# A four-layer gated cross-attention kernel: the first attention prepared three batches deep with squares on ScalarE and scaling on GpSimd, and two mixtures reordered

## The reference, cut to what matters

```python
x = x + tanh(g_xattn[0]) * L0_xattn(ctx, layernorm(x), mask)   # 4 heads of 64, layer norms, RMS norms
x = x + tanh(g_ffn[0])   * L0_ffn(layernorm(x))                # top-1 of 8 experts, hidden 1024
...
x = x + tanh(g_xattn[3]) * L3_xattn(layernorm(x), ctx)
x = x + tanh(g_ffn[3])   * L3_ffn(layernorm(x))                # 64 slots, GRU update, slot attention
```

```python
xn, ln = layernorm(ctx), layernorm(layernorm(x))        # 361 and 100 rows
q = ln @ Wq.T
k, v = split(concat([xn @ Wkv.T, ln @ Wlkv.T]))         # 461 rows: keys from context and from x
qn = q / rms(q) * q_gain * 64**-0.5                     # rms per row and head of 64
kn = k / rms(k) * k_gain
out = softmax(where(mask, qn @ kn.T, -max)) @ v @ Wo.T + bo
```

## Time and profile before

| | us |
|---|---|
| median of three runs | 2035.22 |
| lowest and highest | 2031.48, 2040.41 |
| the profiled execution: its own time | 2037.1 |
| the profiled execution: its span, first to last instruction | 2035.2 |
| PE busy in the span | 1688.3 (83%) |
| DVE busy | 1009.2 (50%) |
| ACT busy | 619.9 (30%) |
| POOL busy | 251.4 (12%) |
| mean granted clock of PE | 0.904 |

### The profile page before, as it was taken

How to read it: one execution, slowest core, us unless ns; L and a number is a source line. 1 busy time by engine, 2 the same in 40 slices (tenths; PEclk the granted TensorE clock), 3 DMA queues, 4 the chain that set the end, 5 groups by cost and what they waited for, 6 DMA issues and landing times.

```text
span 2035.2 us, 30717 instructions
## 1 busy us (share of the span) xinstructions
PE 1688.3 (83%) x9090; PEld 1185.3 (58%) x9090; DVE 1009.2 (50%) x3131; ACT 619.9 (30%) x1731; POOL 251.4 (12%) x299
## 2 busy tenths in 40 slices
PE   2888888873699993999999989979997996887676
PEld 1555545543589982666666657757775534665454
DVE  3677777754122221444444443644444555775663
ACT  1343334321222221333333323223332003443232
POOL 2222222211200003000000000110000011112000
PEclk9899889785799996999999988989998996998787
DMA  3000000700788851000000000010000003000001
GB/s 89 13 14 12 12 12 13 221 1 29 258 305 319 303 215 49 12 12 11 11 11 11 6 1 8 17 32 22 22 22 1 13 20 119 27 27 1 0 1 33
DMA packets 88389, 117.17 MB, mean 58 GB/s; under 512 B 16418, under 2 KB 80130, under 8 KB 83202
## 3 DMA queue, kind: packets, MB, share of 16 engines
q1 hardware_dynamic: 86274, 113.06, 17.2%
q0 software_dynamic: 2048, 3.29, 0.6%
HBM read 104.51 MB, written 8.52 MB: 56 GB/s over the span
## 4 chain that ended last, share of the span: by engine, by line
PE 56%; issue 21%; DVE 8%; POOL 7%; ACT 3%; DMA 1%; SPq 1%; DVEq 1%; POOLq 0%; ACTq 0%
PE bank L1811 7%; PE bank L2061 6%; PE bank L1918 5%; PE bank L2158 5%; PE bank L1868 5%; PE bank L1892 4%; PE bank L2071 4%; POOL work L645 3%; PE bank L1946 3%; PE bank L1903 3%; PE bank L1860 3%; PE bank L2113 2%; PE bank L2129 2%; PE bank L2245 2%; POOL work L638 1%
## 5 line engine op out<-in xcount | busy, mean ns | idle before, releaser
L812 ACT ACTIVATE work<-bank,work 100x361 f32<-100x361 f32 (+1 forms) x272 | 159.5, 590 | 276.7 <-DVE work L1185 225.8
L1918 PEld LDWEIGHTS bank<-work 128*100 128x100 f32 x1760 | 191.4, 174 | 76.1 <-issue 35.2
L1194 DVE COPY work<-bank 128x300 f32<-128x300 f32 (+1 forms) x272 | 125.6, 490 | 187.9 <-PE bank L1903 187.6
L1918 PE MATMUL bank<-work 128*100 128x64 f32 (+1 forms) x1760 | 198.1, 262 | 22.7 <-DVE work L1194 22.6
L2061 PEld LDWEIGHTS bank<-work 128*128 128x128 f32 x1280 | 148.4, 194 | 1.9 <-ACT work L910 0.9
L2061 PE MATMUL bank<-work 128*128 128x128 f32 x1280 | 148.7, 277 | 0.5 <-ACT work L910 0.5
L1185 DVE TENSOR_REDUCE work<-bank 100x1 f32<-100x361 f32 x208 | 101.9, 528 | 87.4 <-PE bank L1892 72.6
L1892 PE MATMUL bank<-work 64*100 64x361 f32 (+1 forms) x512 | 142.2, 558 | 2.0 <-ACT work L802 1.1
L1903 PE MATMUL bank<-ident,work 100*128 100x100 f32 x880 | 112.7, 259 | 29.2 <-ACT work L812 28.4
L638 POOL TENSOR_TENSOR work<-work,neg_half 100x1 f32<-100x1 f32 x96 | 53.2, 554 | 593.9 <-DVE work L1132 593.8
L1903 PEld LDWEIGHTS bank<-ident,work 100*128 100x128 f32 x880 | 89.8, 147 | 56.8 <-ACT work L812 49.9
(11 more groups left out here) (286 smaller groups left out, 2824.0 us busy)
## 6 DMA issues: line engine op xcount, KB each, us to landing
work<-in_F_w SPq DMA_DIRECT2D x60, 1024.0 KB, 6.4
work<-in_ctxT SPq DMA_DIRECT2D x64, 135.4 KB, 2.2
work<-in_ctx SPq DMA_DIRECT2D x32, 192.0 KB, 2.4
sorted_x<-zeros SPq DMA_DIRECT2D x1, 2560.0 KB, 10.0
work<-sorted_x SPq DMA_DIRECT2D x20, 128.0 KB, 6.2
work<-in_F_b SPq DMA_DIRECT2D x20, 128.0 KB, 6.7
sorted_y<-work SPq DMA_DIRECT2D x20, 128.0 KB, 6.3
work<-in_ctx SPq DMA_DIRECT2D x32, 78.8 KB, 2.2
```

The source lines that it names most:

```text
L812: nc.scalar.activation(pr[:, 0:NK], S_bank[k][0:T, 0:NK], ACT.Exp, bias=nmax[k][0:T, :], accum_out=rsum[j][0:T, h:h + 1]).then_inc(s.exped ...
L1194: nc.vector.tensor_copy(PT[k][:, 0:CH, :], PT_bank[k][:, 0:CH * T].rearrange("p (c t) -> p c t", c=CH)).then_inc(s.probs_copied.sem, 1)
L1918: ins = nc.tensor.matmul(to, PT[k][:, c, :], values, start=(c == 0), stop=(c == CH - 1))
```

## The change

1. **First attention.** `three_deep` takes the place of `pipelined` there: in `first_attend(t)` steps 0 to 7 belong to batch t+2 and steps 8 to 10 to batch t+1; the norms on DVE and POOL belong to batch t+3. The order of the steps is the tuple `AHEAD`. `V` now holds four batches (`vv0`). Heads go in pairs, 0 with 1 and 2 with 3. ACT squares each chunk from PSUM before it copies it. POOL multiplies each chunk with its power right behind the power. DVE keeps the sums and their scaling.
2. **Routed mixture.** The down product of tile i-1 stands in tile i behind piece f = 1, its bias on DVE behind piece 2; `AC` has two buffers; the next rows are turned behind piece 4. SP asks for the rows of a tile before its W1. For the first two tiles W1 of both and W2 of the first are asked before SP waits for the scatter.
3. **Slot mixture.** `in_waves` takes the place of the rounds: stage s of pair u runs in wave s + 9u on every engine. `pick` works on one pair, and both additions of the logits' bias (`biased`) stand before all picks. The same instructions are issued otherwise.

The core of the diff:

```diff
-PAIRS = (0, 4, 2, 0)
-EARLY = ((0, 1), (0, 1, 2), (0, 1, 2), (0, 1, 2))
+PAIRS = (2, 4, 2, 0)
+EARLY = ((0, 1, 5), (0, 1, 2), (0, 1, 2), (0, 1, 2))
 GROUPS = (
-    ((2, 3, 4), (5, 6, 7), (), (8, 9, 10)),
+    ((2, 6, 8, 3), (4, 9, 10, 7)),
...
+AHEAD = (0, 1, 5, 2, 6, 8, 3, 4, 9, 10, 7)
+ALONE = tuple(n for n in AHEAD if n < 8)
+APART_BY = 9
+PICKED = 7
...
+def three_deep(eng, attend, finish):
+    for t in range(4):
+        attend(t, t)
+    with eng.Fori(1, B // 4 - 1) as i:
+        for q in range(4):
+            attend(4 * i + q, q)
+    for t in range(B - 4, B):
+        attend(t, t % 4)
+    finish(B - 1, 1)
+def in_waves(stages):
+    for wave in range(max(stages) + APART_BY * (B // 2 - 1) + 1):
+        for u in range(B // 2):
+            if wave - APART_BY * u in stages:
+                stages[wave - APART_BY * u](u, u % SLOTS_AT_ONCE)
...
 # GpSimd, first attention
                         nc.gpsimd.tensor_tensor(rr[j][:, 4 * k:4 * k + 4], rr[j][:, 4 * k:4 * k + 4], neg_half[:, 0:4],
                                                 ALU.pow).then_inc(s.rqk.sem, 1)
+                        wait_for(pool, s.rqk, 5 * t + n + 1)
+                        nc.gpsimd.tensor_tensor(v, v, r, ALU.mult).then_inc(s.qk_scaled.sem, 1)
...
 # ScalarE, steps 4 to 7
+                            nc.scalar.square(QKsq[:, k, :], src[:, 0:D])
                             nc.scalar.copy(QK[j][:, k, :], src[:, 0:D])
-                            ins = nc.scalar.copy(vv(0, j)[:, k, :], src[:, D:2 * D])
+                            ins = nc.scalar.copy(vv0(q)[:, k, :], src[:, D:2 * D])
...
 # TensorE, first attention
+                def first_attend(t, q):
+                    j = q % 2
+                    started = not (isinstance(t, int) and t == 0)
+                    scores(t, j, 0)
+                    scores(t, j, 1)
+                    ahead(t, q, EARLY[0][:2])
+                    if started:
+                        o_turn(t - 1, 1 - j)
+                    ahead(t, q, EARLY[0][2:])
+                    for p in range(PAIRS[0]):
+                        probs_turn(t, j, 2 * p)
+                        probs_turn(t, j, 2 * p + 1)
+                        if p == 0:
+                            if started:
+                                project(t - 1, 1 - j)
+                            scores(t, j, 2)
+                            scores(t, j, 3)
+                            ahead(t, q, GROUPS[0][0])
+                        else:
+                            ahead(t, q, GROUPS[0][1][3:])
+                        weigh(t, q, 2 * p)
+                        weigh(t, q, 2 * p + 1)
+                        if p == 0:
+                            ahead(t, q, GROUPS[0][1][:3])
...
 # TensorE, routed mixture, in the loop over f
-                    if more:
-                        rows_turn(i + 1, 1 - j)
+                        if f == DOWN_AFTER and not (isinstance(i, int) and i == 0):
+                            down(i - 1, 1 - j)
+                        if f == 4 and more:
+                            rows_turn(i + 1, 1 - j)
...
 # SyncE, routed mixture, the first two tiles
+                first_layer(tile0, 0)
+                first_layer(tile1, 1)
+                second_layer(tile0, 0)
+                sp.wait_ge(s.scattered, 16 * B)
+                rows(0, 0)
+                rows(1, 1)
+                second_layer(tile1, 1)
...
 # slot mixture: VectorE and TensorE
+                in_waves({0: pick, 2: alpha, 4: pooled_and_alpha, 8: rz_in, 10: rz_done, 12: slots_new, 16: v_done, 18: masked,
+                          21: attn_copy, 23: y_stats, 25: y_norm, 29: values_done, 33: residual})
+                in_waves({3: sums_and_alpha, 5: pooled_turn, 7: gru_in, 13: s_turn, 15: qkv, 17: attn, 20: attn_turn, 22: comm,
+                          26: y_turn, 28: values, 30: mixed, 32: out_rows})
```

More of the change, by code:

```diff
@@ L45 @@
 STEPS0 = -(-B * T // P)
+DOWN_AFTER = 1
 E1, HID1 = 8, 128
@@ L373, in flamingo_kernel @@
         SG = [area.take(P) for _ in range(2)]
-        AC = area.take(HID0 // P, P)
+        AC = [area.take(HID0 // P, P) for _ in range(2)]
         YR = [area.take(D) for _ in range(2)]
@@ L547, in routed_experts, with rows, first_layer @@
                 sp.wait_ge(s.places, PLACED)
[L549 to L555 removed]
+                def rows(i, j):
+                    sp.dma_start(TR[j][:, :], sorted_x[bass.ds(i * P, P), :]).then_inc((s.rows_in0, s.rows_in1)[j], 16)
+                def first_layer(one, j):
                     for c in range(2):
@@ L719, in one @@
                                             ).then_inc(s.rstd_y, 1)
-                for u in range(B // 2):
-                    one(u, u % SLOTS_AT_ONCE)
+                in_waves({24: one})
                 end(pool)
@@ L879, in finish, with ahead @@
                         v_copy(t, j)
-                pipelined(act, prepare, attend, finish)
+                def ahead(t, q, steps):
+                    for n in steps:
+                        if n < 8 and follows(t, 2):
+                            step(t + 2, (q + 2) % 4, n)
+                        if n >= 8 and follows(t, 1):
+                            step(t + 1, (q + 1) % 4, n)
+                def first_attend(t, q):
+                    j = q % 2
+                    ahead(t, q, EARLY[0][:2])
+                    exp(t, j, 0)
+                    exp(t, j, 1)
+                    if not (isinstance(t, int) and t == 0):
+                        o_copy(t - 1, 1 - j)
+                    ahead(t, q, EARLY[0][2:])
+                    ahead(t, q, GROUPS[0][0][:2])
+                    exp(t, j, 2)
+                    exp(t, j, 3)
+                    ahead(t, q, GROUPS[0][0][2:] + GROUPS[0][1])
+                if L == 0:
+                    for n in ALONE:
+                        step(0, 0, n)
+                    for n in AHEAD:
+                        step(1 if n < 8 else 0, 1 if n < 8 else 0, n)
+                    three_deep(act, first_attend, finish)
+                else:
+                    pipelined(act, prepare, attend, finish)
                 end(act)
```

308 lines of the change are left out of this document (180 added, 128 removed).

## The result

The changed kernel takes 1970.74 us (median of 4, 1969.45 to 1976.53), the kernel before beside it 2037.82: a ratio of 0.9684, 95% interval 0.9656 to 0.9711. The forecast was 1949, its range 1915 to 1985.

The account below looks back on a forecast made before the run. TensorE and VectorE, each about four-fifths busy and waiting for the other inside one batch, were taken to set the first attention's 23.7 us. First attention -66, routed mixture -12, slot mixture -8: -86 from 2035.2 to 1949 us, range 1915 to 1985.

Parts of the forecast that it names:

- other two rivals: First attention: new depth not used, batch near 23, 2010 us, chance 0.06; clock stays down, 2065 at 8 batches, 0.04.
- First attention, batch 20.6: First attention: a batch falls from 23.7 to 20.6 us, taken between 20.9 by busy time plus waits and 20.3 walked.
- four walked waits: First attention, PE: waits before step 5 (1.65 to 2.85), step 3 (9.4 to 10.3), step 10 (15.05 to 15.95), step 4 (0.2).
- Prologue 56.5: First attention's start: batches 0 and 1 prepared first, so batch 0's scores move from 51.1 to about 56.5 us.
- +14 us of low clock: First attention: 14 us added for stretches at the lower clock, less than today's because PE's gaps are fewer.
- GpSimd 0.73 (0.42 to 1.38): First attention: price of each scaling of 128x256 moved to POOL, 0.73 us taken, ends 0.42 and 1.38.
- The covers: First attention: POOL at 12 or 15.5 us and DVE at 16.0 with two waits stay below the batch time.
- the rival's 26 us: First attention: squares bind ACT, holding five PSUM banks 0.37 us longer; 26 us come back, 1975 us; chance 0.14.
- Heads side by side, 1.0 to 1.1: First attention: heads 2 and 3 run together, one pass less on PE, 1.0 us a batch (1.10 with its tail).
- Routed mixture: Routed mixture: a tile falls from 11.41 to 10.9 us at DMA 0.92, -12 us, ends -4 and -15.
- Slot mixture, 14.4 a block: Slot mixture: walked block of nine waves takes 14.4 us; -8 us in all, ends -25 and +10.
- the clock stays up: With no gap over 1.3 us, the 14 us of low clock and some of the slots' go: 1930 us; chance 0.14.

Follow-up runs that it names:

- the parted scores: Changed kernel with a transpose put between the scores of heads 2 and 3 in the first attention: 1990.1 us, ratio 0.977.
- alone: The kernel before with only the routed mixture's part of the change: 2024.1 us, ratio 0.995 to the kernel before.
- TensorE kept busy: Changed kernel with three added products of 512 columns, results discarded, in each slot mixture block ahead of the mixing products: 1959.7 us, ratio 0.965.

## Why the prediction was right where it was, and where it failed

The result lies in the range, and at the edge of the forecast's own range (1925 to 1972); the likeliest value is 22 us too low. That the total fits is in part luck: the first attention gave 7.6 us more than forecast and the slot mixture, at +21, came out beyond both of its stated ends (-25 and +10), 29 us worse than forecast. The prediction's other two rivals did not come: a batch is 20.1 us, so the new depth is used, and the clock did not stay down. By steps:

- *First attention, batch 20.6.* Measured 20.0 to 20.1. The walk by start times (20.3) was nearer than the count of busy time plus waits (20.9). Of the four walked waits three are there, 0.82, 0.65 and 0.66 us for the walked 1.2, 0.9 and 0.9; the 0.2 ahead of step 4 is not.
- *Prologue 56.5.* The step that failed in this stage: the first scores are at 65.5, +9 us. I had costed the prologue by GpSimd's chain and an estimate for the turns and projections, with PE at full speed. In it four of PE's rows of context products take 3.4 to 3.8 us against 1.98 later, and PE waits 0.7 to 0.9 us for ScalarE ahead of each of the four (timeline of PE, changed kernel):

```profile
53.76 3.78 PE L1920 MATMUL bank<-L_WkvT,work 96*128 96x512 f32 x4 [0.68 <-ACT work L861]
```

  The granted clock is 0.51 from 50 to 60 us, but it reads 1.00 from 30 to 40 us and 0.98 from 40 to 50, where the first two of the four slow rows lie; that contradiction stays open. How many rows are slow differs by execution: with the same first attention the first scores start between 61.7 and 65.7 us in five traces. So some 5 of the 9 us are there in the best of them, the rest comes and goes.
- *+14 us of low clock.* It did not come: clock 1.00 from the first scores to 347 us. From 65.5 to the scores of batch 14 at 347.4 there are 281.9 us where I had 288, and from there to the end some 31 where I had 27. Together 9 - 6 + 4 - 14 = -7, the -73.6 against -66.
- *GpSimd 0.73 (0.42 to 1.38).* Measured 0.61. The covers held: DVE is 75% busy, and no single operation of it from 90 to 190 us takes more than 0.74 us.
- *Squares on ScalarE.* That the wait for step 6's bank includes the square was in the walk, rightly, and so the rival's 26 us did not come on top. But the cost was there: the stage was 10.4 us longer than with the squares on VectorE, in a choice that the walk had already accepted as given.
- *Heads side by side, 1.0 to 1.1.* 1.2, by the parted scores.
- *Routed mixture.* 10.84 a tile for 10.9, DMA 0.91 for 0.92, -11.3 (alone -12.7) for -12. Right in size and in mechanism.
- *Slot mixture, 14.4 a block.* The step that made the miss. The walk was right for a clock of 1.00: with the clock held and the same order the block measured 14.47. What it left out is what its own wait does to the clock. I named "+10 if the clock stays at its lower level in the steady blocks" as an end and did not ask what would put it there. The answer stood in the walk: the picks ahead of the gates leave PE idle once a block, 2.49 us, and the clock falls for 6 us each time. By the starts of the picks the 29 us between forecast and result are these: the first picks 20.5 us into the stage for 17.7 (+2.7); the three blocks of the fill 44.5 us for 36 (+8.5); the five full blocks 85.5 for 72 (+13.5); the drain to the last residual 27.4 for 25.5 (+1.9); the rest, some 2 us, I had taken off for overlap. The fill is 44.5 us in the kernel with TensorE kept busy too, at a granted clock of 0.69 in both, since its added products begin only with the first mixing product. What the fill would take at a clock of 1.00 no run shows.
- *Rival "the clock stays up".* Half of it came: in the first attention, where PE waits 0.65 to 0.82 us at a time and is 90% busy, no burst of low clock lay between the first scores and 347 us. In the slot mixture the opposite happened, and I had priced the two stages with one rule. The Trainium skill, "TensorE: Matmul & The Clock Gate", section "Why this matters for your kernels", names long idle gaps as what brings the clock down. The slot mixture does not agree that they must be long: the clock fell in every full block with an idle time of 2.49 us, and in 4 of 15 blocks whose longest was 0.86 us.

## What to carry over

Price an idle time of TensorE at its own length plus what the clock costs behind it: here 2.5 us of idle time cost some 3 more. When work is reordered into waves, look at what stands in each engine's queue right ahead of the product that the tensor engine waits for, and move whatever nobody waits for, such as the picks, into the place where that engine waits itself. An engine that is half idle can still be the wrong one to add work to, if its instructions are what frees the banks: the squares cost the stage 10 us more on ScalarE, 53% busy with them, than on VectorE, 88% busy with them.

## What was not expected of the hardware

- The clock's fall depends on more than one idle time: blocks with the same order, the same 59 products and the same waits of 0.86 and 0.48 us ran at 1.00 or at 0.79 within one execution. What decides between the two I cannot tell.
- In every kernel with the new first attention one batch, the ninth, is 2 to 8 us longer. DVE starts it late, with no wait that the trace shows. Its idle time there is put down to "issue" (timeline of DVE, changed kernel):

```profile
225.83 0.42 DVE L1295 TENSOR_TENSOR work<-bank,work 100x256 f32<-100x256 f32 x1
229.14 0.70 DVE L1267 CUSTOM_DVE_ANT_0 bank<-bank,work 100x512 f32<-100x512 f32 x1 [2.88 <-issue]
```

The ninth batch is where the loop of four batches jumps back for the only time, which fits; it was not tested. The 2.9 us cost 1.8 in the changed kernel, and 7.9 with the scores parted, where the granted clock is 0.50 from 245 to 255 us, behind the late start. Kernels with the same first attention lose between 1.8 and 3.7 us there.
- GpSimd's multiplication of 128x256 with a broadcast operand takes 0.61 us, less than its 100x256 addition at 0.73; the nearest row gave an upper bound here and not the value.
